# Five steps of an even phase moved: sigmoid, packing and joining of u, joining of the routing weights

## The reference

```python
def ffn(x):                                  # used twice, with the same weights
    shared = silu(xf @ Ws_up) @ Ws_down
    aff = xf @ centroids.T                   # 64 experts
    _, idx = top_k(aff + expert_biases, 8)
    w = sigmoid(take_along_axis(aff, idx))
    w = w / (sum(w) + 1e-8)                  # placed in cw[token, expert]
    h = silu(einsum('td,edf->etf', xf, W_up))          # every expert, 64 x (128 -> 64)
    y = einsum('etf,efd->etd', h, W_down)
    return shared + einsum('etd,te->td', y, cw)

def attn(u):                                 # u is shifted by one token both ways
    xf = concat(u[:1], u[1:] @ WB.T);  xb = concat(u[1:] @ WBf.T, u[-1:])
    gamma = sigmoid(xf @ w1.T + xb @ w2.T + b)
    return gamma * (xf + xb) + (1 - gamma) * u

x = x + 0.5 * ffn(layernorm(x))
x = x + attn(layernorm(x))                   # u = layernorm(x1)
x = x + 0.5 * ffn(layernorm(x))
```

## Time and profile before

| what | us |
|---|---|
| median of 3 runs | 769.28 (769.12 to 769.4) |
| the profiled execution | 770.05 |
| its span, first to last instruction | 767.8 |
| PE busy | 755.7 (98%) |
| DVE busy | 631.9 (82%) |
| ACT busy | 633.4 (82%) |
| POOL busy | 538.6 (70%) |

### The profile page before, as it was taken

How to read it: one execution, slowest core, us unless ns; L and a number is a source line. 1 busy time by engine, 2 the same in 40 slices (tenths; PEclk the granted TensorE clock), 3 DMA queues, 4 the chain that set the end, 5 groups by cost and what they waited for, 6 DMA issues and landing times.

```text
span 767.8 us, 11832 instructions
## 1 busy us (share of the span) xinstructions
PE 755.7 (98%) x3393; PEld 617.3 (80%) x3393; DVE 631.9 (82%) x1399; ACT 633.4 (82%) x1220; POOL 538.6 (70%) x555
## 2 busy tenths in 40 slices
PE   8999999999999999999999999999999999999998
PEld 5788878878887888788887888878888788888786
DVE  6788989888779786897969889687887888688875
ACT  7998779778898888879888699887988878777885
POOL 3795656677868877688676787777887777564453
PEclk9999999999999999999999999999999999999999
DMA  8000000011101112001110012001020011000000
GB/s 293 17 1 14 2 15 7 15 42 35 37 12 29 41 36 46 13 14 48 52 23 14 14 48 55 20 14 44 17 55 20 14 41 35 15 2 0 15 1 14
DMA packets 63070, 23.57 MB, mean 31 GB/s; under 512 B 49344, under 2 KB 61888, under 8 KB 63040
## 3 DMA queue, kind: packets, MB, share of 16 engines
q1 hardware_dynamic: 63040, 23.21, 11.6%
HBM read 9.05 MB, written 2.10 MB: 15 GB/s over the span
## 4 chain that ended last, share of the span: by engine, by line
PE 73%; DVE 10%; ACT 9%; issue 5%; POOL 2%; DMA 1%; ACTq 0%; POOLq 0%; DVEq 0%; SPq 0%
PE y_ps L1094 12%; PE y_ps L1096 11%; PE y_ps L1095 11%; PE up L1094 11%; PE up L1096 11%; PE up L1095 11%; ACT g_hi L703 3%; ACT up L665 3%; DVE gated L921 2%; DVE g_lo L930 2%; DVE up L921 1%; POOL g_lo L443 1%; ACT normed L791 1%; DVE stats L850 1%; PE side L1154 1%
## 5 line engine op out<-in xcount | busy, mean ns | idle before, releaser
L443 POOL TENSOR_TENSOR g_lo<-gated,g_hi 128x512 fp32r<-128x512 f32 x255 | 333.5, 1308 | 164.6 <-ACT g_hi L703 164.0
L665 ACT ACTIVATE up<-up 128x512 f32<-128x512 f32 x512 | 300.0, 586 | 62.6 <-PE up L1096 61.4
L921 DVE TENSOR_TENSOR gated<-up,cw 128x512 f32<-128x512 f32 x256 | 175.1, 684 | 78.4 <-ACT up L665 74.1
L1094 PE MATMUL y_ps<-g_hi,wd_hi 128*128 128x512 f32 x512 | 203.6, 398 | 2.9 <-POOL g_lo L443 2.5
L1094 PE MATMUL up<-x_hi,wu_hi 128*128 128x512 f32 x512 | 200.4, 391 | 1.4 <-DVE g_lo L930 1.3
L921 DVE TENSOR_TENSOR up<-up,cw 128x512 f32<-128x512 f32 x256 | 176.8, 691 | 29.0 <-ACT up L665 27.5
L1096 PE MATMUL y_ps<-g_hi,wd_lo 128*128 128x512 f32 x512 | 199.6, 390 | 0.0
L1095 PE MATMUL y_ps<-g_lo,wd_hi 128*128 128x512 f32 x512 | 199.5, 390 | 0.0
L1095 PE MATMUL up<-x_lo,wu_hi 128*128 128x512 f32 x512 | 199.4, 389 | 0.0
L1096 PE MATMUL up<-x_hi,wu_lo 128*128 128x512 f32 x512 | 199.4, 389 | 0.0
L930 DVE TENSOR_TENSOR g_lo<-up,g_hi 128x512 fp32r<-128x512 f32 x256 | 174.4, 681 | 10.4 <-ACT g_hi L703 9.2
(11 more groups left out here) (161 smaller groups left out, 555.7 us busy)
## 6 DMA issues: line engine op xcount, KB each, us to landing
x_in<-in_x SPq DMA_DIRECT2D x8, 256.0 KB, 2.8
wu_raw<-in_w_up SPq DMA_DIRECT2D x4, 512.0 KB, 8.5
wd_raw<-in_w_down SPq DMA_DIRECT2D x4, 512.0 KB, 9.3
x_res<-in_x SPq DMA_DIRECT2D x8, 256.0 KB, 2.7
out<-out_sb SPq DMA_DIRECT2D x7, 256.0 KB, 2.2
mix<-in_mix SPq DMA_DIRECT2D x1, 389.0 KB, 7.8
n_turned_halves<-n_halves SPq DMA_TRANSPOSE x17, 2.7
out<-out_sb SPq DMA_DIRECT2D x2, 128.0 KB, 2.1
```

The costliest lines, as they stand in the source:

```text
L443: nc.gpsimd.tensor_tensor(g_lo[:, i, :], gated[:, t // 2 % ORING, :], g_hi[:, i, :].bitcast(fp32), ALU.subtract).then_inc(lo_done[1], 1)
L665: nc.scalar.activation(up[i][:, :], up[i][:, :], ACT.Silu).then_inc(silu_done, 1)
L921: nc.vector.tensor_tensor(gated[:, t // 2 % ORING, :] if t % 2 else up[i][:, :], up[i][:, :], cw[ph.q][:, :], ALU.mult).then_inc(gate_done, 1)
L1094: nc.tensor.matmul(o, a[0], b[0], start=start, stop=False)
```

## The change

Only the table of the even loop phases is changed. `sig` goes from slot 15 to slot 17, behind the two halves of `norm1_act`. The first half of `u_pack` goes from slot 15 to 16, which is behind the low part of tile 15. `u_join` goes from slots 19 and 21 to 20 and 22, where each half stands behind a low part (of tile 19, of tile 21). The second half of `cw_join` goes from slot 31 to 30, in front of the root `rstd2`.

```diff
 AT_STEADY_B = {
     "x_split": 1, "aff": 4, "aff_pack": 4, "sh_silu": 5, "sh_high": 6, "sh_low": 12, "aff_join": 9,
-    "sig": 15, "bias": 15, "max": 16, "take": 18, "gate": 20, "sum": 21, "inv": 23, "cw_pack": (24, 25), "cw_join": (29, 31),
+    "sig": 17, "bias": 15, "max": 16, "take": 18, "gate": 20, "sum": 21, "inv": 23, "cw_pack": (24, 25), "cw_join": (29, 30),
     "y": 2, "y_join": (5, 7), "x1": 7, "stat1": (8, 9), "aggr1": 10, "rstd1": 10, "shift1": 13, "norm1_act": (14, 15),
-    "xu": 23, "u_pack": (15, 17), "u_join": (19, 21),
+    "xu": 23, "u_pack": (16, 17), "u_join": (20, 22),
```

## The result

The changed kernel takes 773.14 us in the median of 5 runs (772.66 to 773.65); the kernel before, run beside it, 769.28 (769.12 to 769.7). The ratio is 1.0049 with a 95% interval of 1.0037 to 1.0061; the medians differ by 3.9 us. The forecast was 771.3 with 769.3 to 773.2, slower.

A forecast was written before the change was run, and what follows sets the result against it. PE, busy 98% of the span, bounds the kernel; only its waits for GpSimd's g_lo can be won. Attention waits 3 x 0.78 + 2 x 0.60, less 5 x 0.29, give +2.1 on 769.28: 771.3 us, range 769.3 to 773.2.

The forecast's parts named there:

- The sigmoid's move: ScalarE, slot 15 to 17: norm's second half, silu behind it and rounding of tile 15 come 0.77 us earlier; silu 18 stays.
- Packing and the first join: GpSimd: low part 15 ends at 415.14, low part 19 starts at 418.84 us, both before PE wants them.
- stalls a and b: PE's waits before the down products of tiles 15 (0.66 us) and 19 (0.16, last two passes 0.34); forecast gone.
- The select held by low part 19: VectorE's select, issued 0.38 us into GpSimd's low part, takes 1.20 us, so gate 21 stays at 420.34.
- Rival 2: The select isn't held; everything from gate 21 on is 0.29 us earlier: 769.9 us, no change; chance 0.17.
- The second join behind low part 21, and a new wait at the attention product: u_mid complete at 423.76; PE waits in slot 25, costing 0.78 us in three passes, 0.60 in the last two.
- Stall d: PE's wait before the down product of tile 31; forecast gone with the weights' join earlier, -0.29 us in each pass.
- The sum: Five passes: 2.34 + 1.20 - 1.45, together +2.1 us on the median of 769.28: 771.3 us.
- Rival 1: The attention product doesn't wait and all three stalls are won: 763.4 us; chance 0.15, including what lies toward no change.
- Rival 3: The wait before tile 31's down product stays, its slack being only 0.1 us: +3.5, 772.8 us; chance 0.10.

The follow-up runs named there:

- sigmoid_only: The kernel before with the sigmoid in slot 17 instead of 15 and nothing else: 765.23 us, ratio 0.9946.
- waits_ahead: The changed kernel with PE's three other waits of the attention product made before the down product of slot 25: 772.07 us, ratio 1.0037 to the kernel before.
- sig_weights_early: The kernel before with the sigmoid in slot 17 and the weights' joins in slots 28 and 29 instead of 29 and 31: 763.91 us, ratio 0.9926.
- join_23: The changed kernel with the second half of joining u in slot 23 instead of 22: 782.95 us, ratio 1.0177 to the kernel before.

## Why the prediction was right, and where its sizes were off

The direction, the order of the steps and the place of the new wait were right; the size was not. The loss is 3.9 us where 2.0 were forecast, and the time lies only 0.06 below the upper end of the range. Two terms were mis-sized to the same side, so that the range held was partly luck.

- **The sigmoid's move**: right. Low part 15 ended at 416.43 less 1.28 = 415.15 (forecast 415.14), and silu 18 kept its place (415.44). sigmoid_only shows the gain it would have brought by itself.
- **Packing and the first join**: right. Low part 19 started at 418.85 in the old frame (forecast 418.84), and stalls a and b are gone.
- **The select held by low part 19**: right in all five passes (1.19 to 1.20 us). The rule of the Trainium skill, page "SBUF — State Buffer", section "SBUF: two separate sides", that whichever of the two starts first keeps the other out for its whole instruction, agrees with the trace here, where the select started 0.38 us behind. The other direction, the select first, agrees with sigmoid_only, where the low part took 1.46. With less than 0.1 us between the two recorded starts it went either way (last section). Rival 2, the select not held, is out.
- **The second join behind low part 21, and a new wait at the attention product**: right in place and in order; `u_mid` was complete at 423.74 in the old frame (forecast 423.76). The term was mis-sized in the handover. I took 0.05 from the join's end to the matmul and it was 0.25, because PE had other wait instructions beside the one that held it (waits_ahead). The product started 0.85 us later than before in the third pass, where the forecast had 0.67 (in the old frame at 423.99, the upper bound of 424.0); over five passes A grew by 3.9 us against 3.0. The gap of about 1.7 us came out only because both its ends moved by 0.2: PE was ready for the product at 422.49 in the old frame and not at 422.3.
- **Stall d**: mis-sized. The prediction booked -0.29 for each pass; the root's first instruction started 0.86 behind the join's start, not 0.69, and PE was 0.02 late and paid its slow step. B, in which I also had +0.11 behind the attention product (it was 0.08), changed by -0.11 on average where the sum had -0.18: -0.5 us instead of -0.9. sig_weights_early shows where the missing part was: the join in front of the root.
- **The sum** by the terms as measured is 3.9 - 0.5 = +3.4 us against +2.1; the spans differ by 3.1, with the first phases, ahead of the change, 0.3 shorter in the profiled execution after. The medians differ by 3.9. The last 0.5 is within the spread of the runs (772.66 to 773.65) and was not settled. (769.28 + 2.1 is also 771.4 and not 771.3.)
- **Rival 1**, all three stalls won, is what the other placings reach: 763.4 was its price, and sig_weights_early has 763.91. It needed `u_mid` to come before PE does, as the prediction said, and the changed table puts it behind. Where the gain of the sigmoid's move went is thus shown: with the joins where they were it is 4.2 us, with the joins moved it turns into a longer wait at another consumer of the same queue.
- **Rival 3**, stall d staying, was half true and no cause of the loss. Its price, 772.8, is the nearest to the measured time, but about half of stall d did go; the rest of the difference is the handover.

## What to carry to other kernels

A wait on the bounding engine that ends with some other engine's queue is not cured by reordering that queue alone: list all consumers of the queue, with the slack of each (here 0.86 us at the attention product), before a step is put behind another. In a chain of engines follow the first engine that is late: moving two ScalarE instructions by two slots cured two stalls that the profile booked to GpSimd. The select and the scaling, VectorE's instructions with two SBUF operands, cost 0.76 to 0.78 us more when they started 0.37 to 0.38 us into a GpSimd instruction of 1.3 us, and moving one step in the tables brought the next such meeting; so look for what such an instruction meets at its new time.

## What the runs showed of the hardware that was not expected

- Gaps of 2.36 to 2.38 us in PE's stream (start to start, join_23) were followed, 1.0 to 1.3 us behind their end, by matmuls at the lower clock in four of five passes (spacing 0.43 instead of 0.23), each costing 1.6 us. A gap of 2.41 us at the same place in the first pass was not, nor were the five of 1.73 to 1.74 us in the changed kernel. This nearly tripled what join_23's extra wait cost: 9.8 us for 3.3 us of waiting. That the gap is the cause is argued from this; no run changed the gap alone.
- Several wait instructions in front of one matmul aren't free even when all but one were met long before: 0.25 us from release to the matmul with the three others there, 0.06 with none.
- VectorE and GpSimd kept each other out in four kinds of meeting: the select started in a low part (1.20 for 0.42), the scaling in xu (1.19 for 0.43), a join in the select (0.97 for 0.77), a low part in the select (1.46 for 1.29). The record of the held instruction includes the time in which it is held, and in these four it ends 0.12 to 0.15 us sooner than the other's end plus its own undisturbed time.
- Where the two start almost together the order of the starts doesn't tell which is held. In the kernel before, a join starts 0.06 to 0.08 us ahead of the select in each loop pass; the select was held in the first three passes (0.90 to 0.91), the join in the last two (1.12, with the select at 0.41 to 0.42).
